# Other step strings for a four-engine schedule written out by hand: a two-layer attention and mixture-of-experts model on one core

## The reference

```python
x = x + _L0_xattn_ref(ctx_1024, ctx_1024, _layernorm(x, axis=-1), ...)   # one head of 256 over the context
x = x + _L0_ffn_ref(_layernorm(x, axis=-1), ...)     # 32 heads of 8, then an expert MLP 256 -> 1024 -> 256
x = x + _L1_xattn_ref(_layernorm(x, axis=-1), ctx_1024, ...)             # attention over the context
x = x + _L1_ffn_ref(_layernorm(x, axis=-1), ...)     # 16 heads of 16, then a top-2 mixture of 8 experts
```

## Time and profile before

| what | us |
|---|---|
| median of 3 runs | 2132.25 |
| lowest, highest | 2129.85, 2133.82 |
| profiled execution, first to last instruction | 2134.7 |
| TensorE busy | 1937.1 |
| VectorE busy | 1347.4 |
| ScalarE busy | 998.0 |
| GpSimd busy | 598.9 |
| one full round | 94.5 |

### The profile page before, as it was taken

One profiled execution on the slowest core, in us unless ns is written; L12 is line 12 of the kernel. 1 busy time (PEld: TensorE's weight loads), 2 busy tenths in 40 slices (PEclk: granted clock), 3 DMA queues, 4 the chain that ended last, 5 costly groups with the idle time before them and its releaser, 6 DMA issues. The chain is left out here.

```text
span 2134.7 us, 37545 instructions
## 1 busy us (share of the span) xinstructions
PE 1937.1 (91%) x13657; PEld 1452.8 (68%) x13657; DVE 1347.4 (63%) x3466; ACT 998.0 (47%) x1956; POOL 598.9 (28%) x490
## 2 busy tenths in 40 slices
PE   5588999999999999999999999998888649999998
PEld 4456666666667666666666666676666428998997
DVE  2436667676766667676666767665765546766764
ACT  1144655555565555565565555554434213433332
POOL 0101131312113031212203131221121126667664
PEclk8679999999999999999999999998989659999999
DMA  5221433525152443515143352414120244344322
GB/s 184 84 84 53 158 102 114 167 91 168 50 167 75 146 132 116 164 62 168 63 158 110 108 175 81 164 52 149 43 90 1 79 133 113 82 115 98 45 40 26
DMA packets 205704, 224.86 MB, mean 105 GB/s; under 512 B 15083, under 2 KB 195248, under 8 KB 205520
## 3 DMA queue, kind: packets, MB, share of 16 engines
q1 hardware_dynamic: 191136, 206.40, 29.2%
q0 software_dynamic: 14384, 16.06, 4.7%
HBM read 150.82 MB, written 72.52 MB: 105 GB/s over the span
## 5 line engine op out<-in xcount | busy, mean ns | idle before, releaser
L1268 DVE TENSOR_REDUCE MX<-bank 128x2 f32<-128x512 f32 x768 | 493.2, 683 | 171.4 <-PE bank L901 169.4
L1517 ACT ACTIVATE PT<-bank 128x512 f32<-128x512 f32 x768 | 416.7, 597 | 254.9 <-PE bank L938 251.3
L901 PE MATMUL bank<-KS,QS 32*128 32x256 f32 (+1 forms) x1536 | 196.7, 335 | 48.8 <-DVE MX L1268 45.8
L938 PE MATMUL bank<-QM,KS 32*128 32x256 f32 (+1 forms) x1536 | 196.3, 334 | 29.6 <-ACT PT L1517 25.5
L953 PE MATMUL bank<-PT,VA 128*32 128x256 f32 x3072 | 213.4, 397 | 9.0 <-ACT PT L1517 8.8
L901 PEld LDWEIGHTS bank<-KS,QS 32*128 32x128 f32 (+1 forms) x1536 | 119.0, 191 | 137.6 <-DVE MX L1268 73.6
L938 PEld LDWEIGHTS bank<-QM,KS 32*128 32x128 f32 (+1 forms) x1536 | 119.8, 191 | 117.3 <-issue 69.4
L1870 ACT ACTIVATE hid<-bank,b1T 128x512 f32<-128x512 f32 x128 | 87.8, 686 | 226.7 <-PE bank L1822 198.9
L746 POOL TENSOR_TENSOR rrB<-uwB,cst 128x4 f32<-128x4 f32 x16 | 16.3, 1018 | 599.7 <-DVE uwB L1237 599.7
L1835 PE MATMUL bank<-W2h,hTh 128*128 128x256 f32 x512 | 142.7, 279 | 0.0
L1835 PE MATMUL bank<-W2l,hTh 128*128 128x256 f32 x512 | 141.4, 276 | 0.0
(11 more groups left out here) (331 smaller groups left out, 3871.1 us busy)
## 6 DMA issues: line engine op xcount, KB each, us to landing
W<-in_L_ffn_w_dram SPq DMA_DIRECT2D x48, 1024.0 KB, 6.9
KS<-k_dram SPq DMA_DIRECT2D x64, 512.0 KB, 5.7
QS<-q_dram SPq DMA_DIRECT2D x64, 512.0 KB, 5.9
k_dram<-qTQ SPq DMA_DIRECT2D x32, 256.0 KB, 2.5
q_dram<-pTQ SPq DMA_DIRECT2D x32, 256.0 KB, 7.1
k_dram<-PRP SPq DMA_DIRECT2D x32, 256.0 KB, 2.6
q_dram<-cTP SPq DMA_DIRECT2D x32, 256.0 KB, 2.6
X<-in_x_dram SPq DMA_DIRECT2D x16, 256.0 KB, 6.6
```

Of the source, the lines that this page charges most:

```text
L901: x = mm(halves(u)[:, r, :], Q[strip, slot, r * P:(r + 1) * P], K[strip, slot, :], start=True, stop=True)
L938: x = mm(halves(2 + u)[:, kc, :], K[strip, slot, kc * P:(kc + 1) * P], QM[strip, slot // 2 % 2, slot % 2, :], start=True, stop=True)
L1268: v.tensor_reduce(MX[:, slot % 4, j, :], halves(u), AX, ALU.max, negate=True).then_inc(h.maxed, 1)
L1517: s_.activation(PT[:, n % 8, :, :], halves(2 + n % 2), ACT.Exp, scale=h.scale).then_inc(h.exp, 1)
```

## The change

Only the strings and their assignment to rounds change. Every new string has each letter as often as the one it replaces, so no instruction is added or removed; the threads, their waits, tiles and DMAs are the same. Rounds 0, 1 and 14 get strings of their own (`SECOND`, `THIRD`, `FOURTH`) in place of `ORDER`; round -1 and rounds 2 to 13 walk the new `ORDER`; rounds 15 to 17 walk the new `EARLY`, `LATE` and `LAST`.

```diff
-ORDER = "QQPPSQPPSQSTPSPESTEPSEVETSVESQESPTSQPSEVSPQSPESPTSQPVSEPQSEPSPEVQTESPQPESVEPPSEQVPSQETPSQEPQEVPSQEVPQTEPEPVEPEQEVQV"
+ORDER = "QQSPPQSPPQTSPQSPESTQPESPPESPTSPSEVSPTESVESPPTSEPQSPEVSEPQSEVPQESVEQTPQSEPSEQVPSEQVPSETPESQVEQSPEQVESPQTPPEQPEVEVEQV"
-EARLY = "QPQPPSPSQSTPSRRSPETERRRRERSVPSQQQERTSEVRSEQTPRSRPRRVSEPRQSPESPPRSTRESVESPESPQEVSPVSPTPQSEQPPESRSPQSPEQTSPEQEVQRERPQVRPRRERRQQTRRRRERPVEPEVVRREPERRVQ"
-LATE = "PRPRSPPSSQTPSPRRSETPEPERRSVSQQQERQPRTPRVRRRSPSPSRQPRERTEPPSSESSQVRQSTPEVPQSSEPTSQQPVEPEQSEPESPQPQQRRRPEPRQVERVEVSQETRSRTPRVRRSSPPERQQVEEVRERRRREVEE"
-LAST = "QPSSPSQTSPEPQSPETPSEVPSTEPSEPQVSQPSPQSSSPQESPSTQEVPEPEVSQVQSEQSPPEPSPEEVSQEQPQQPVSPQEPTEEPPSEQVVPVQTPESSPVETETQVEEE"
+SECOND = "SPTSEQEQSPQEETEVVSSSQTSSTSPQSSEQPSQPSEEPTSPESQPVPESEVVPSPETPPPSPESQQPEPVSEVQSEQTSQEQQVSPPEQSPEPPVETQEVEQPPEVPPPEPQV"
+THIRD = "SVSQSSQVSSESPSPTQPPQTPESETPSTPQSPSPQSEVPTESPPPPPQEESEPEQPESPQVEVQSETPPSVESPSEPQTQSQEQPEVQSPEQVSEQPESVPTEPEQPEVEVEQV"
+FOURTH = "QQSPPQSPPQTSPQSEPSQETPSVESPPTSEPSPTESPPSEVSEPTESPVSEPQESVPESQPTSEQVSEPPQSVQEPQVSEPTQSEPESQPVEQSEPVSEQPTQPQEPEVEVEQV"
+EARLY = "RSPPSPSPTSRPEQSRPETRSPREVSRETPERRSRVESQPRRSPTRSPQRRPESRVQQQQPTSEPESRQSPVESEPSVPQESTPSEQSVESPQRSPQPESTQPQSPQERVERQVERPPRRQERRRETRRRRPVEQVREPERPQEVRVR"
+LATE = "RRPSPPSPSPTSEPETRRPSREPPRESRRQVPRQTSRQQPERVRRPESRPPTRPQQEVSEVSSSESRSSPQPQVSQPVQVESQPSEVPEQTPPVEQESQPQERRRQETESRQPRPRERERRRRREETQQSSEPPRVVRRRSVESPTE"
+LAST = "SSSPTQQSPPESETSQEPVSETSQQPEPVQETSEPVEQPPVEESVSVVSTQSPSQPEPQPESQEPEESVVPTPPQPEQQQSPETSEVQSEPPPQSPPEPSEQESPVEEVTPQSSP"
...
-    round_(0, 0, p=False, d=False)
-    round_(1, 1, d=False)
-    for r in range(2, n - 3, 2):
-        round_(r, 0)
-        round_(r + 1, 1)
-    round_(n - 2, 0)
+    round_(0, 0, p=False, d=False, order=SECOND)
+    round_(1, 1, d=False, order=THIRD)
+    for r in range(2, n - 2):
+        round_(r, r % 2)
+    round_(n - 2, 0, order=FOURTH)
```

## The result

The changed kernel takes 2061.22 us in the median of four runs (2058.43 to 2067.89). The kernel before, run beside it, takes 2133.03 us (four runs, 2129.85 to 2141.33). The ratio is 0.966, with a 95% interval of 0.964 to 0.969. The direction was right and the size was not: 28 us less were forecast and some 72 came. The profiled execution after is the shortest of its four runs, so differences between the two profiles come out some 6 us larger than that of the medians.

The account below looks back on a forecast made before the run. TensorE's list of steps, busy 91%, was taken to bound the kernel. Terms of -20.4 - 6 + 9 - 2 - 1 - 5 - 3 = -28.4 us led from the 2132.25 us median to 2104, range 2079 to 2133.

Parts of the forecast that it names:

- The price of a change of division: Full rounds 2 to 13: 0.19 us per array division change on TensorE, nine fewer a round, 20.4 us off.
- The rival of half price: Whole kernel: only the 0.09 us at a step's end goes away per change, giving 2116 us; chance 0.12.
- the count: TensorE's strings: division changes fall from 81 to 72 a full round, 1277 to 1163 overall; 32-row pairs cancel at five.
- The waits in a full round: Rounds 2 to 13: TensorE waits shrink by 0.5 us a round, 6 us in twelve; bounds 2 off, 1.5 on.
- The knot on VectorE: Full round, 14th to 16th S step: VectorE has some 6.6 us of work against TensorE's 4.6.
- the first rival: Full rounds: idle time falls 2 us instead of 0.5 and the fetch comes in time, giving 2077 us; chance 0.15.
- The moved fetch: Start of rounds after the width-16 fetch queues behind a put: TensorE waits 0.7 us each, 9 us in 13 rounds.
- The slower rival: Moved fetch at a higher price: 13 waits of 2.9 us use up the gains; 4 us each gives 2147; chance 0.10.
- Round 0: Round 0 with SECOND: earlier, better separated S steps against five more division changes, net 5 us off, bounds 0 and 10.
- Round 1: Round 1 with its own string: three fewer division changes and a little less waiting, 1 us off.
- From round 14 to the layers' end: Round 14: 2 us off before its fetch wait; rounds 15 to 17: 3 off, bounds 12 off and 10 on.
- the signs of being wrong: A round's waits far from 4 us, fetch wait above 2.3 us, or rounds 15 to 17 moving over 12 us.

Follow-up runs that it names:

- the wide pair: Changed kernel plus a 256-column matmul in the middle of each scheduled product, with 128 rows or with 32: 2153.15 and 2305.31 us.
- fetch first: Changed kernel with SyncE alone issuing the width-16 fetch ahead of the width-8 query put again: 2044.24 us, and 2046.39 when run a second time.
- the experiment with the short distance: Kernel with SyncE's width-16 fetch ahead of the put again, plus A.s moved behind the fourth S step in ORDER: 2056.5 us.
- the late fetch in the kernel before: Kernel before, with SyncE alone issuing the width-16 fetch after the width-8 query put: 2192.92 us, ratio 1.027.

## Why the prediction was wrong, and where it was right

**The price of a change of division** (0.19 us, 9 fewer a round, 20.4 us) was right: the wide pair gives 0.195 and so 21 us. The rival of half price falls. The drain of about 128 cycles that the page TensorE: Matmul & The Clock Gate of the Trainium skill states, in Step-by-step: what each phase is for, an estimate of 53 ns at 2.4 GHz, is not the price of a change here; the measurement is nearly four times that. One part of the count was off: five pairs of 32 rows on different strips stand in both strings, but in a round before (round 9) only four of them ran together, because in the fifth the S step waited. After, all five did.

```profile
944.89 0.50 PE L938 MATMUL bank<-QM,KS 32*128 32x256 f32 x4
945.62 0.50 PE L901 MATMUL bank<-KS,QS 32*128 32x256 f32 x4 [0.23 <-DVE MX L1268]
```

That is, by an estimate from the earlier trace rows, another 0.23 us a round (0.67 - 0.44), which the prediction had let cancel.

**The waits in a full round** were the largest step that failed. The prediction took off 0.5 us a round (6 us in twelve) with bounds of 2 off and 1.5 on. With the fetch out of the way (fetch first against before), a stage sum falls by 53 to 59 us; less 21 for the changes, 32 to 38 us are left for the waits and what goes with them, 2.7 to 3.2 a round. Visible idle time accounts for 24 to 28 us of it. Two steps of the working failed:

- The knot on VectorE from the 14th to the 16th S step was expected to eat most of the gain. VectorE did fall behind there, but TensorE didn't have to wait for it. TensorE's S steps 16 and 17, and the maxima of the first of the two on VectorE, after:

```profile
894.07 0.50 PE L903 MATMUL bank<-KS,QS 32*128 32x256 f32 x4
...
896.43 1.28 DVE L1270 TENSOR_REDUCE MX<-bank 128x2 f32<-128x512 f32 x2
...
898.44 0.40 PE L903 MATMUL bank<-KS,QS 32*128 32x256 f32 x4
```

The maxima end at 897.71, 3.6 us behind their S step's start, and still 0.7 before the next S step. I had set 6.6 us of VectorE's work against the 4.6 of TensorE's between the 14th and the 16th step, and had not looked at the 17th, which comes 4.4 us behind the 16th. VectorE was still at that work when the 16th step ran, and had caught up before the 17th. A queue that falls behind makes nobody wait if it has caught up when its next reader comes.

- The idle time was thought to stay. The visible idle of rounds 2 to 13 is 45.0 us before and 17.5 and 21.5 with the fetch first, 24 to 28 us less, so 2.0 to 2.3 a round, what the first rival had. And even that is not all: the shortest full round goes from 94.4 to 89.4 us, 5.0 less, of which 1.75 are changes and about 2.1 visible waits. The last 1.1 us stand in no wait; they are busy time (90.8 us of such a round before, 87.8 with the fetch first). The pair that now runs together gives 0.23 of them. A record ahead of a wait also counts as busy to its modelled end, 0.50 us for an S or E step that takes 0.43 when the next one follows; with nine such waits in round 9 before and three with the fetch first, that is an estimate of 0.4 us. The rest, half a microsecond, stays open.

That distances decide whether an S step waits was right, and the experiment with the short distance shows it: a distance of 1.0 us in place of one above 1.9 brings a wait of 0.96.

**The moved fetch** was right as a mechanism and its sign, but too cheap. Forecast were 0.7 us a round and 8.4 in rounds 2 to 13. By exchanging it alone it is 16 to 26 us there, 1.4 to 2.2 a round, inside the bounds but near their upper end, and 16.5 in the whole time. The step that failed is the last one of its working. Issue and flight had led to a wait of 0.8 to 2.3 us, and the trace bears that out: an issue 3.8 us ahead, a flight of 6.1, and waits of 0.9 to 2.9 us, 1.5 in the mean. The sum then took 0.7, below the low end of that range, for two reasons that the runs do not bear out. The flight did not get shorter (6.1 us in the median, and 5.2 to 5.5 with the fetch first), and the waits behind a late first S step did not shrink, as the late fetch in the kernel before shows. That experiment also shows a price the prediction didn't have: 1.6 us a round of lower clock behind waits of 2.6 to 3.3 us. In the changed kernel the clock fell so behind one wait, that of 2.88 us in round 6. The slower rival, which needed 2.9 us in each of 13 rounds, met that price in a single round at most (0.9 to 2.9 us in rounds 2 to 13 after, 18 us in all).

**Round 0** was forecast at 5 off with bounds of 0 and 10, and gave 13.7. Its row, against the earlier trace rows:

```profile
PE bank L903 <- DVE MX L1270: 7.3, 8, 1.7
```

S steps wait 4.1 us less, E steps 3.7 less (4.9 to 1.2), an E step's wait for QM from VectorE is gone (1.4), and all idle time goes from 20.7 to 10.5. I looked at one row of waits, the longest, and took back less than half of it; the others gave more than it did. The remaining 3.5 us are busy time: 54.65 to 51.13 us for the same matmuls, at a granted clock of 0.66 before and 0.72 after. These are in part scatter: in the seven kernels here with SECOND and the matmuls as they are, the clock of this round lay between 0.65 and 0.77 and its length between 59.8 and 64.1 us, at 9.6 to 11.4 us of idle time; in the three with the old string it was 0.66 and 75.4 to 76.0 us. Five more changes of division cost nothing that could be seen beside it.

**Round 1** was forecast at 1 off and gave 6.3. Its idle time falls from 7.2 to 3.3. This is the same omission: only the three changes were priced and the waits were called "a little less".

**From round 14 to the layers' end** 4.3 off were forecast and 19.7 came; behind round 14 it is 15.4, above the bound of 12. The S steps' waits between 1397 and 1640 us are

```profile
PE bank L903 <- DVE MX L1270: 9.5, 13, 1.5
PE bank L903 <- DMA QS<-q_dram: 6.3, 2, 5.5
```

so the 16.8 of the earlier trace rows nearly halved, and a single wait of 5.5 us for a fetch is new. What was set against the gain, R's first step ahead of everything, did not show up as a wait: VectorE was through with it at 1405.39 and then idle until the first S step of round 15 gave it work. The stage scatters widely. In the seven kernels with the new strings there it took 369 to 385 us with 73 to 82 us idle, in the three with the old ones 386 to 396 with 84 to 91 idle. Of the 19.7 us between the two profiles, 7.5 are less idle time (84.1 to 76.6); the rest is busy time, at a granted clock that differs from run to run (0.82 to 0.88 in the ten). No experiment takes the strings of the ends apart.

**The sum.** Forecast: -28.4. By stages -78.1 in the profiled execution. Two of the signs of being wrong that the prediction named came true: the fetch's wait was above 2.3 us in round 6, and rounds 15 to 17 moved by more than 12. Rounds 2 to 13 add 19 to the miss (waits 26 to 32 more than forecast, the fetch 8 to 18 less), the ends 9, 5 and 15, and round -1's scatter 3. The forecast had the price of the countable part, changes of division, to within some 6%, and treated everything that had to do with waits as small. That was where most of the gain lay.

## What to carry to other kernels

Where one engine walks a list that others feed, price two things apart: what each item costs beside its neighbours, and the distance between steps that wait for the same feeder; here a distance below the feeder's latency was paid in full, though TensorE was 97% busy. Sum all the waits of a stage, not the longest row, and where an engine falls behind, look whether it has caught up when its next reader comes before you call it a wait. When you have worked out a range for a wait, take a value inside it. Whenever steps are put in another order, look at each queue by itself: here one load behind an unrelated put took back 16 us of 92, and letting SyncE alone keep the old order for those two steps gives the fastest version found, at 2044 to 2046 us.

## What the runs showed of the hardware

- One change of array division costs 0.195 to 0.202 us, measured with 38 more of them in a round and 256 columns each. With one-column matmuls on both sides of the comparison it came out at 0.12 to 0.14, and the control then paid 0.22 us for each of its added matmuls; which of their parts overlap was not tested.
- A load issued behind a put on the same queue flew 6.1 us in the median, and 5.2 to 5.5 issued ahead of it (twelve loads in each run). In the kernel before with the fetch late the one of the round shown went out 1.1 us ahead of the round's start and flew 5.3, so there its place in the queue cost by the issue alone.
- Single full rounds are 2 to 3 us longer at a mean granted clock of 0.96, with as little idle time as their neighbours. Two rounds in a row, after, with the columns of the earlier trace rows:

```profile
389.40:482.60 93.20, 91.06 (x688) 66.55 (x684) 64.69 (x172) 53.86 (x110) 20.16 (x18) 0.96 0.37 123
482.60:573.20 90.60, 87.98 (x689) 64.55 (x685) 64.60 (x172) 53.63 (x110) 20.15 (x18) 1.00 0.39 128
```

  Idle are 2.1 and 2.6 us of them, so the engine had not paused more in the longer one. What differs is one stretch of 6.8 us, 71.9 us into the round, in which the granted clock is 0.50:

```profile
450.00:461.30 11.30, 11.20 (x106) 8.09 (x99) 9.16 (x26) 6.76 (x15) 3.48 (x4) 1.00 0.09 25
461.30:468.10 6.80, 6.73 (x33) 4.76 (x26) 4.23 (x9) 3.57 (x8) 5.87 (x5) 0.50 0.21 78
```

  TensorE was busy for 11.20 of the 11.30 us ahead of it, in good part with steps of 32 rows and, 2.8 us before the fall, with D2.lg, a product of eight columns. In the seven kernels here with the new ORDER and the matmuls as they are, the clock fell 70 to 72 us into 20 of 84 full rounds, and nowhere else but at the wait for QS in five rounds, which waited 1.7 to 2.9 us. It happens in the kernel before as well, once (96.3 us at 0.98 against 94.5), at another place of the round. Why it falls there in some rounds and not in others that walk the same steps was not found.
